# A four-layer decoder on one core: early float8 weights, one-variance norms, full-row biases, and causal masks moved from PE to DVE

## The reference

```python
# l0f: the feed-forward block of layer 0 begins with a norm of a norm, then causal attention
h = layernorm(x);  xn = rmsnorm(h) * ln1          # 32 query heads, 8 key heads of 64
h = h + causal_attention(xn);  y = rmsnorm(h) * ln2
p = softmax(y @ gate_w);  top 2 of 8 experts, their weights renormalised
# l1a: a gated long convolution (Fourier transform written as products), l1f: float8 feed-forward
wq = float8(w); gate, up = xq @ wq_gate, xq @ wq_up; x + float8(act(gate) * up) @ wq_down
# l2a: causal differential attention, 64 query heads of 8 wide; l2f: norm of a norm,
# then causal attention with 16-wide heads, then 7 experts
s = q @ k.T / sqrt(hd);  s = where(k_pos <= q_pos, s, -inf);  softmax(s) @ v
```

## Time and profile before

| | |
|---|---|
| three runs | 2653.11, 2655.5, 2662.68 us; median 2655.5 |
| the profiled execution | 2658.09 us, its span 2656.9 us |
| busy | PE 2081.8 us (78%), DVE 1519.9 (57%), ACT 1089.7 (41%), POOL 1048.7 (39%) |
| stages by time (us from the start) | start and l0a projection 0 to 78, l0a attention to 327, l0x end and l0f norm 343 to 376, l0f attention 388 to 760, router and experts to 1206, l1a 1211 to 1311, l1f 1326 to 1452, l2a 1453 to 1802 (attention 1494 to 1787), l2x to 2172, l2f 2173 to 2440 (attention 2220 to 2312), l3 to 2657 |

### The profile page before, as it was taken

One profiled execution on the slowest core, in us unless ns is written; L12 is line 12 of the kernel. 1 busy time (PEld: TensorE's weight loads), 2 busy tenths in 40 slices (PEclk: granted clock), 3 DMA queues, 4 the chain that ended last, 5 costly groups with the idle time before them and its releaser, 6 DMA issues. The chain is left out here.

```text
span 2656.9 us, 35337 instructions
## 1 busy us (share of the span) xinstructions
PE 2081.8 (78%) x12705; PEld 1444.6 (54%) x12752; DVE 1519.9 (57%) x2932; ACT 1089.7 (41%) x2195; POOL 1048.7 (39%) x1084
## 2 busy tenths in 40 slices
PE   5667759999956888876524988887999978888887
PEld 2333346667646777763302555445687765555446
DVE  6877655545444555544678655544466554456546
ACT  3245625464523434433166144452343434422433
POOL 2766617455636665650254233341232222322000
PEclk8756679999977999997756978888999989979778
DMA  3222110000014445421001000002000000012000
GB/s 140 72 56 59 49 51 8 23 12 16 5 40 155 149 153 163 147 82 44 9 39 37 2 3 2 3 3 103 1 1 1 1 1 1 3 66 107 2 1 17
DMA packets 49150, 121.38 MB, mean 46 GB/s; under 512 B 5553, under 2 KB 18353, under 8 KB 47185
## 3 DMA queue, kind: packets, MB, share of 16 engines
q1 hardware_dynamic: 47440, 114.92, 13.3%
q0 software_dynamic: 1536, 4.20, 0.5%
HBM read 103.50 MB, written 14.55 MB: 44 GB/s over the span
## 5 line engine op out<-in xcount | busy, mean ns | idle before, releaser
L1796 POOL TENSOR_SCALAR l0f_probs<-l0f_probs,l0f_tot 128x128 f32<-128x128 f32 (+1 forms) x256 | 201.6, 806 | 141.8 <-DVE l0f_tot L1743 141.2
L2018 PE MATMUL ps<-l0f_xh,l0f_wh 128*128 128x256 f32 x480 | 149.3, 311 | 49.6 <-DVE l1x_dBu L649 28.4
L1262 DVE TENSOR_REDUCE l2a_a_max<-ps 128x6 f32<-128x768 f32 x128 | 119.4, 953 | 87.5 <-PE ps L1114 86.9
L3114 POOL TENSOR_TENSOR l2x_probs<-l2x_probs,l2x_rc 128x512 f32<-128x512 f32 x64 | 66.5, 1039 | 254.7 <-DVE l2x_rc L3015 254.7
L1318 POOL TENSOR_SCALAR_AFFINE_SELECT l2a_a_probs<-l2a_a_probs 128x256 f32<-128x256 f32 (+1 forms) x192 | 88.3, 484 | 170.4 <-ACT l2a_a_probs L1224 148.3
L2133 POOL TENSOR_TENSOR l0f_wl<-l0f_raw,l0f_wh 128x1024 fp32r<-128x1024 f32 x60 | 141.8, 2375 | 17.8 <-ACT l0f_wh L2058 17.8
L2019 PE MATMUL ps<-l0f_xl,l0f_wh 128*128 128x256 f32 x480 | 141.0, 294 | 0.0
L2020 PE MATMUL ps<-l0f_xh,l0f_wl 128*128 128x256 f32 x480 | 141.0, 294 | 0.0
L1667 ACT ACTIVATE l0f_probs<-ps,l0f_neg 128x128 f32<-128x128 f32 (+1 forms) x256 | 104.3, 424 | 87.2 <-DVE l0f_neg L1733 87.2
L674 POOL TENSOR_TENSOR l1x_y<-l1x_y,l1x_hc 128x512 f32<-128x512 f32 x64 | 80.8, 1283 | 129.0 <-DVE l1x_hc L665 129.0
L2955 ACT ACTIVATE l2x_probs<-ps,l2x_neg,l2x_rs 128x256 f32<-128x256 f32 x128 | 71.0, 559 | 145.5 <-DVE l2x_neg L3005 145.4
(11 more groups left out here) (728 smaller groups left out, 5858.3 us busy)
## 6 DMA issues: line engine op xcount, KB each, us to landing
l0f_raw<-in_e_l0f SPq DMA_DIRECT2D x60, 512.0 KB, 4.1
l0x_bc<-scratch_bc SPq DMA_DIRECT2D x32, 512.0 KB, 4.8
l0f_raw_d<-in_e_l0f SPq DMA_DIRECT2D x60, 256.0 KB, 3.8
scratch_rows<-zero SPq DMA_DIRECT2D x1, 3840.0 KB, 18.8
l0f_xb<-scratch_rows SPq DMA_DIRECT2D x15, 256.0 KB, 4.5
scratch_results<-l0f_yb SPq DMA_DIRECT2D x15, 256.0 KB, 4.8
l0f_slab<-in_g_l0f SPq DMA_DIRECT2D x8, 448.0 KB, 3.5
l1f_raw<-in_w_l1f SPq DMA_DIRECT2D x1, 3072.0 KB, 9.9
```

Of the source, the lines that this page charges most:

```text
L1262: dve.tensor_reduce(M[:, 2 * half:2 * half + 2, j, :], src.rearrange("p a (c n) -> p a c n", c=NB_), AX.X, ALU.max).then_inc(*unit_max.tick())
L1796: last = pool.tensor_scalar(pr[:, u % 3, a, r], pr[:, u % 3, a, r], tot[:, u % 3, qt, a:a + 1], None, ALU.mult)
L2018: pe.matmul(out, hi, xh[:, j % 2, c, :], start=c == 0, stop=False)
```

## The change

Five edits. (1) The causal mask is no longer added on PE. DVE's `tensor_tensor_reduce` adds a mask block to the scores in PSUM, writes them back there, and gives the row's maximum; it is issued four times for each unit, two of 128 columns and two of 256. The products L1114 and L1607, the reductions L1262 (in the causal uses), L1730 and L1731, and `join` go. (2) The float8 rounding of l1_ffn's weights moves into `l1_attention` as class `Early`: four transfers (3 MB) on SP ahead of `dft`, six chunks in each phase between the existing work of ACT, DVE and POOL; mid and round are all on POOL. In the second phase ACT does chunk 6 before it copies the frequencies, 7 to 9 between them and 10, 11 after; DVE scales 6 before K's copies, 7 and 8 after them, 9 after the products of f = 0, 10 and 11 among its last operations; POOL does 6 and 7 before its products and 8 to 11 after. SP stores the result (bf16, 1.5 MB) to `scratch_l1f` before the last barrier, and l1_ffn loads it back. `Turned` writes float8 itself. (3) `NormTwice` gets both norms from one set of statistics, with five operations on 8 or 16 columns and one root. (4) Biases lie in a full block of 128 rows of which the first holds the bias, and are added with a product over 128 rows instead of one. (5) The router of l0f leaves out the division by the softmax's sum, and `start` makes fewer constants.

```diff
+    def masked_max(self, scores, half, out):
+        at = 0 if half else P
+        return self.dve.tensor_tensor_reduce(scores, scores, self.mask[:, at:2 * P], 1.0, 2 * MASKED, ALU.add, ALU.max, out)
...
 start:
-    dve.tensor_copy(k.kb[:, 128:384], k.kf[:, 368:624])
-    dve.memset(k.kb[:, 384:512], 1.0)
-    dve.tensor_copy(k.kb[:, 512:768], k.kf[:, 624:880])
+    dve.memset(k.kb[:, 128:512], 1.0)
...
+class NormTwice:
+    def dve(self):
+...
+        for i in range(NT):
+            dve.tensor_scalar(self.xn[:, i, :], self.src[:, i, :], k.mv[:, i, 0:1], self.both[:, i:i + 1],
+                              ALU.subtract, ALU.mult).then_inc(*k.sig("normed").tick())
+    def dve_first(self):
+        for i in range(NT):
+            k.dve.tensor_scalar(self.h[:, i, :], self.src[:, i, :], k.mv[:, i, 0:1], self.r[:, 0, i:i + 1],
+                                ALU.subtract, ALU.mult).then_inc(*k.sig("v").tick())
...
 project_pe:
-        last = k.pe.matmul(out, k.ones[0:1, :], bias, start=False, stop=True)
+        last = k.pe.matmul(out, k.ones, bias, start=False, stop=True)
...
 small_attention, unit:
-                if causal:
-                    for a in range(2):
-                        diagonal = banks[:, a, :].rearrange("p (q n) -> p q n", n=S)[:, :, 0:P]
-                        last = pe.matmul(diagonal, k.identb, k.mask_qk.unsqueeze(1).to_broadcast([P, 2, P]), start=False, stop=True)
...
 small_attention, largest:
-                src = ring("unit", b, u)[:, :, 0:384] if causal else ring("unit", b, u)
-                dve.tensor_reduce(M[:, 2 * half:2 * half + 2, j, :], src.rearrange("p a (c n) -> p a c n", c=NB_), AX.X, ALU.max).then_inc(*unit_max.tick())
-            def join(b):
-                dve.wait_ge(*unit_max(NU * (b + 1)))
-                dve.tensor_tensor(Mj[:, :, :], M[:, :, :, 1], M[:, :, :, 2], ALU.max).then_inc(*joined.tick())
+                if causal:
+                    for a in range(2):
+                        for qt in range(2):
+                            last = k.masked_max(src[:, a, qt * P:P + qt * S], qt, M[:, 2 * half + a, j, qt:qt + 1])
...
 l0_ffn (and l2_ffn alike):
-                ln.dve(False, 1, collected=True)
-                k.dve.wait_ge(*normed(8))
-                rn.dve(True, 2)
+                norm.dve()
                 turn.dve()
+                norm.dve_first()
...
 l0f_attention, score:
-                for i, (unit, mask) in enumerate(((k.identb, k.mask_qk), (k.ident_swap, k.mask_swap))):
-                    for r, bank in halves:
-                        diagonal = bank[:, 0:512].rearrange("p (q n) -> p q n", n=S)[:, :, 0:P]
-                        last = pe.matmul(diagonal, unit[r, :], mask[r, :].unsqueeze(1).to_broadcast([64, 2, P]), start=False, stop=i == 1)
 l0f_attention, largest:
-                dve.tensor_reduce(m[:, 0, :], banks[:, :, 0:P], AX.X, ALU.max).then_inc(*vc.tick())
-                dve.tensor_reduce(m[:, 1, :], banks[:, :, P:P + S], AX.X, ALU.max).then_inc(*vc.tick())
+                for a in range(2):
+                    for qt in range(2):
+                        k.masked_max(banks[:, a, qt * P:P + qt * S], qt, m[:, qt, a:a + 1]).then_inc(*vc.tick())
...
 router:
-            dve.tensor_reduce(sm[:, :], pr[:, :, :], AX.X, ALU.add).then_inc(*v.tick())
-            dve.reciprocal(sm[:, :], sm[:, :]).then_inc(*v.tick())
-            dve.tensor_tensor(pr[:, :, :], pr[:, :, :], bc(sm), ALU.mult).then_inc(*v.tick())
...
+class Early:
+    CHUNKS, PIECES = 12, ((0, 1), (1, 4), (4, 8), (8, 12))
+    def act(self, i):
+        self.k.act.wait_ge(*self.ready[i])
+        self.quant.act(self.col(self.raw, i), i % 3, i - self.first)
+    def dve(self, i):
+        self.k.dve.wait_ge(*self.ready[i])
+        self.quant.dve_scale(self.col(self.raw, i), i % 3, i - self.first)
+    def pool(self, i):
+        n = i - self.first
+        self.quant.pool_mid(i % 3, n)
+        self.quant.pool_round(self.col(self.raw, i), i % 3, n)
+        self.quant.pool_out(self.col(self.w8, i), i % 3, n)
+    def store(self):
+        self.k.sp.wait_ge(*self.quant.done.now())
+        self.k.sp.dma_start(self.k.kept8, self.w8[:, :]).then_inc(*self.kept.tick())
+        self.k.sp.wait_ge(*self.kept.now())
...
 l1_attention, phase 1 (HERE = 6):
+                early.act(0)
                 for i, (n, dst, off, d, hf) in enumerate(JOBS):
...
+                    if i % 2 == 1 and i // 2 + 1 < HERE:
+                        early.act(i // 2 + 1)
...
+                early.dve(0)
+                early.dve(1)
                 for d in range(2):
                     dve.wait_ge(*taken(2 * d + 2))
                     dve.tensor_scalar(q[:, d], qp[:, d, :, 2:2 + S], w["cqw"][:, d, 2:3], w["cqb"][:, d:d + 1], ALU.mult, ALU.add).then_inc(*v.tick())
+                    if d == 0:
+                        early.dve(2)
+                        early.dve(3)
+                    else:
+                        early.dve(4)
+                        early.dve(5)
...
+            for i in range(HERE):
+                early.pool(i)
...
+            early.store()
             k.barrier()
...
l1_ffn:
-        k.weights("l1f", "l1f", raw)
+        k.load("l1f", w8[:, :], k.kept8)
-            norm, turn = Norm(k, c2, "l1f_", xn, k.x), Turned(k, xT, xn)
+            norm, turn = Norm(k, c2, "l1f_", xn, k.x), Turned(k, x8, xn, saturate=False)
-            dve.tensor_copy(x8[:, :, :], xT[:, :, :], saturate=False)
-            quantise_weights(k, quant, w8, raw, 6144)
```

More of the change, by code:

```diff
@@ L95, in pk, with first_row @@
         return np.ascontiguousarray(np.concatenate(parts, 1))
+    def first_row(b):
+        return np.concatenate([b.reshape(1, -1), np.zeros((P - 1, b.size), np.float32)])
     def ssm(p):
@@ L197, in __init__ @@
         self.identb = self.kb[:, 0:128]
[L198 to L202, removed]
+        self.mask = self.kf[:, 368:624]
         self.w = {}
@@ L357, in act @@
             if self.scale is None:
-                k.act.copy(out, k.ps[:, g, :]).then_inc(*xa.tick())
+                k.act.copy(out, k.ps[:, g, :], **self.cast).then_inc(*xa.tick())
             else:
@@ L368, in dve @@
             if self.scale is None:
-                k.dve.tensor_copy(out, k.ps[:, g, :]).then_inc(*xd.tick())
+                k.dve.tensor_copy(out, k.ps[:, g, :], **self.cast).then_inc(*xd.tick())
             else:
@@ L1109, in unit @@
                         last = pe.matmul(banks[:, a, at:at + w], QT[z][r, j, qt * P:(qt + 1) * P], KT[z][r, hs.kj(j), 0:w],
-                                         start=qt == 0, stop=not causal and qt == 1)
-                if causal:
-                    for a in range(2):
-                        diagonal = banks[:, a, :].rearrange("p (q n) -> p q n", n=S)[:, :, 0:P]
-                        last = pe.matmul(diagonal, k.identb, k.mask_qk.unsqueeze(1).to_broadcast([P, 2, P]), start=False, stop=True)
+                                         start=qt == 0, stop=qt == 1)
                 last.then_inc(*unit_ps.tick())
@@ L1141, in score @@
                         last = pe.matmul(bank[:, i * w:(i + step) * w], KT[z][r, hs.kj(js[i]), kt * P:(kt + 1) * P],
-                                         QT[z][r, js[i]:js[i] + step, q0:q0 + w], start=i == 0, stop=(late or not causal) and i + step == len(js))
-                if causal and not late:
-                    for a in range(2):
-                        diagonal = ps[:, 4 + 2 * (n % 2) + a, :].rearrange("p (j n) -> p j n", n=w)[:, :, 0:P]
-                        last = pe.matmul(diagonal, k.identb, k.mask_kq.unsqueeze(1).to_broadcast([P, len(js), P]), start=False, stop=True)
+                                         QT[z][r, js[i]:js[i] + step, q0:q0 + w], start=i == 0, stop=i + step == len(js))
                 last.then_inc(*scored.tick())
@@ L1871, in step @@
             dve.wait_ge(*v.now())
-        dve.tensor_scalar(self.before[:, :], k.kf[:, 368:496], 0.0, None, ALU.is_lt)
+        dve.tensor_scalar(self.before[:, :], k.kf[:, 496:624], 0.0, None, ALU.is_lt)
         src = pr
@@ L3196, in at_dve @@
                 def at_dve():
-                    ln.dve(False, 1, collected=True)
-                    dve.wait_ge(*normed(8))
-                    rn.dve(True, 2)
+                    norm.dve()
                     turn.dve()
+                    norm.dve_first()
                     for t in range(NT):
```

442 lines of the change are left out of this document (233 added, 209 removed).

## The result

The changed kernel took 2671.6 us in the median of 20 runs (2659.6 to 2680.1), the kernel before 2654.4 (2650.6 to 2669.2). The ratio is 1.0058, 95% interval 1.0043 to 1.0074: slower, by a small but clear 0.6%. I had forecast 2638, faster. The profiled execution has a span of 2677.1 us.

| stretch | before | after | difference | forecast |
|---|---|---|---|---|
| start, to l0a's norm | 15.1 | 13.4 | -1.7 | -1.5 |
| l0a, norm to first score | 64.1 | 61.1 | -3.0 | 0 |
| l0a, first score to l0f's norm | 279.5 | 276.4 | -3.1 | 0 |
| l0f's norms, to its first weights product | 20.4 | 16.4 | -4.0 | -4.1 |
| l0f attention, to the router | 395.0 | 400.6 | +5.5 | -9 |

What follows compares the result with a forecast made beforehand. PE was taken to set the pace in l0f and l2a attention, with waits on DVE's maxima and POOL. Terms summed to -18.5 us (l1_ffn -43.8, l2a +26, phase 1 +13 among them), giving 2638, range 2588 to 2695.

Steps and rivals of the forecast that it cites:

- Net +3.3 us per batch at 1.6: l2a attention: longer DVE maxima outweigh saved PE products if four operations cost 1.6 us; times eight batches, +26 us.
- rival (d): l2a: PE stops more often and is granted the lower clock more, +20 us there, 2658 in all; chance 0.05.
- +0.73 per unit: l2a and l2f: DVE's added time per unit, four masked operations at 1.6 us against one reduction at 0.87.
- my own walk: l2a: one batch followed by its rows, giving about -1 us at 1.2, +3.3 at 1.6, +8 at 2.26.
- an operation of 2.26 us: Masked attentions: four operations cost 2.26 us; l2a +65, l2f +18, l0f +8, 2708 in all; chance 0.22.
- The sign of being wrong: Masks on DVE: forecast wrong if masked_max costs under 1.3 or over 1.95 us, or l2a's stops don't follow it.
- Forecast +6 by DVE: l2f attention: same working as l2a, 4 batches of 8 units, +6 us, from -6 to +18.
- l0f, "-9": l0f attention: PE's saved mask products outweigh DVE's added time, -9 us, from -18 to +8.
- The chain through POOL: l0f: maxima, exponentials, inversion, POOL, then turn; changes by +0.23 us per unit while PE's work falls by 0.32.
- Biases, "0": Bias products: PE streams the same columns whatever the rows, 0 us; bound 4 us from some 40 products.
- Phase 2 itself: l1_attention phase 2: two POOL chunks and early.dve(9) each add 0.8 us, +1.6; up to +5 if cover is gone.
- Phase 1: l1_attention phase 1: early weights' POOL operations hold DVE, plus four scalings of 0.42 us; +13 us, from 9 to 20.

Runs made afterwards that it cites:

- e4: Changed kernel with small_attention's maxima from one reduction over unmasked scores, as cheap as before, and no mask products: 2636.5 us, ratio 0.9900 to the kernel before.
- e6: e4 plus two PE products per unit that add zeros, nothing masked: 2605.3 us, ratio 0.9789 to the kernel before.
- e8: e6 with four zero products per unit; in l0f, DVE's new operation plus four zero products on PE: 2627.7 us, ratio 0.9865 to the kernel before.
- e7: e6 with zero products of 128 columns instead of 256: 2642.3 us, ratio 0.9937 to the kernel before.
- e3: Changed kernel plus two zero-adding PE products per causal unit of small_attention, shaped like the old mask products: 2684.8 us, ratio 1.0086 to the kernel before.
- e10: Changed kernel plus four zero products per unit of small_attention, masks still on DVE: 2645.6 us, ratio 0.9941 to the kernel before.
- e9: e4 with l0f's mask left out altogether, two reductions as before and no mask products; single run: l0f 389.1 us.
- e5: Kernel before with full-row biases alone: 2651.3 us, ratio 0.9974 to the kernel before.

## Why the prediction was wrong

The sum failed at the masks. Point by point:

- **l2a, the step that failed:** "Net +3.3 us per batch at 1.6". I walked the batch with the products' durations of before, that is with their clock of before. The clock is not a constant of the stage. I had the mechanism as rival (d), priced at +20 and at a chance of 0.05, for l2a only, and took the range's upper end from DVE's price. Two errors lay against each other. DVE's price was mis-sized: +0.73 per unit, measured +0.39. By my own walk almost nothing would be lost at 1.26 us, and the stage lost 57. That 2671.6 lies within 2588 to 2695 is luck: the upper part of the range stood for an operation of 2.26 us, which the trace denies. The sign of being wrong that I had named, `masked_max` under 1.3, did come true, at 1.26, but a cheap operation was to make the kernel faster.
- **How the 57 divide.** As a rough estimate, busy PE time times granted clock gives products at full clock: 230 us before, 178 after, so some 52 us of work went. At 0.88 the rest would take 203 us, and it took 283: the clock took back about 80. The measure isn't exact, since the clock is a mean over the whole stretch: the first two zero products per unit raise it by 50 us (e4 to e6), the next two by only 27 (e6 to e8). PE's idle time rose from 37 to 73. The two aren't independent, since slow products delay the maxima. The runs side by side, length and clock, l2a / l2f:

| products per unit | cheap DVE | dear DVE |
|---|---|---|
| none | 318.3 at 0.68 / 105.2 at 0.74 (e4) | 356.0 at 0.63 / 107.3 at 0.76 (after) |
| two zeros of 128 columns | 328.6 at 0.73 / 100.7 at 0.85 (e7) | |
| two of 256 columns | 298.7 at 0.88 / 94.1 at 0.96 (before), 301.2 at 0.87 / 94.1 at 0.96 (e6) | 363.4 at 0.71 / 115.7 at 0.75 (e3) |
| four of 256 columns | 314.8 at 0.90 / 97.1 at 0.96 (e8) | 339.5 at 0.86 / 101.9 at 0.97 (e10) |

The DVE step alone is 25 us of l2a where the clock holds (e8 to e10), 38 where PE is light (e4 to after), and 62 where it tips the clock over at unchanged PE work (e6 to e3). So each half of the change loses the clock by itself. At the measured +0.39 my walk would charge the DVE step some 42 us, which the saved products nearly cancel; measured at a good clock it is 25, and what the walk lacked is that removing the products does not save 45 us but costs 20 (e4).
- **l2f:** the same, 94 to 107. Forecast +6 by DVE; the pair e8 and e10 gives +4.8 for that at a good clock. Removing the products alone gives +11 (e4, clock 0.96 to 0.74), and the DVE step on top of it 2.
- **l0f, "-9":** wrong by itself, and not by the clock (0.97 and 0.95). The forecast set the new 1.6 against the old 1.05, which had the wait before the scaling in it. By the like measure the operation cost 1.41. The chain through POOL was said to take back more than half of the saving; it takes back more than all. No products and cheap DVE give -6 (e9, 389.1). DVE's new operation puts 10 on top: seven profiles have it without the products, six at 398.6 to 400.7 and one (e7) at 395.0. Zero products beside it add 5 (e8). +0.36 us per unit in the chain became +0.16 per unit on the stage, while 0.32 of products gave back 0.09. PE now waits 20.9 us for POOL where the earlier trace rows had 12.8:

```profile
PE ps L1641 <- POOL l0f_probs L1821: 20.9, 15, 2.7
```

- **Biases, "0":** wrong, -7 (e5), beyond the bound of 4 as well. I had said that only the columns count; the one-row products themselves and the full products of the same tiles were slower. Why one row is slower stays open.
- **Right:** the rounding's removal (-43.8, measured -43.6), the norms (-4.1 and -6.0; -4.0 and -6.2), `start`, and the store hidden behind phase 2 (issued at 1306.8, landed after 5.1 us; the last operation ahead of the barrier ended at 1317.4). Phase 2 itself (+1.6; +1.3) came out partly by luck: the biases give back 1.5 in the same stretch (e5), so the early weights cost some 2.8 there. Phase 1 (+13; +11.5) was near, and its mechanism holds. It rests on DVE and POOL taking turns; DVE's and POOL's rows of phase 1 (answer to the earlier trace rows):

```profile
1226.91 2.29 DVE L2465 SCALAR_TENSOR_TENSOR l1a_kv<-l1a_kp,w_l1a,l1a_kv 128x1024 f32<-128x1024 f32 x1
...
1249.60 1.22 DVE L2468 TENSOR_TENSOR l1a_kv<-l1a_kv,l1a_v 128x1024 f32<-128x1024 f32 x1
```

```profile
1214.21 1.26 POOL L2349 TENSOR_TENSOR l1f_early_M<-l1f_early_M,l1f_early_I 128x512 f32<-128x512 f32 x1 [8.88 <-ACT l1f_early_I L2320]
...
1228.09 2.24 POOL L2349 TENSOR_TENSOR l1f_early_M<-l1f_early_M,l1f_early_I 128x512 f32<-128x512 f32 x1
```

DVE's operation of 1.28 us (L2327 before) takes 2.29 beside POOL's, and POOL's of 1.26 takes 2.24. What the prediction lacked: the one-input scalings of the early weights, priced at 0.42, also take longer beside POOL's operations. Five of the twelve took 1.37 to 1.51 us, some 5 us more in all:

```profile
1217.36 1.51 DVE L2327 TENSOR_SCALAR l1f_early_M<-l1f_early_raw 128x512 uint32<-128x512 uint32 x1
```

What stays open is how the chip decides. In l2a the granted clock doesn't follow the columns in proportion (e4, e7, e6: 0.68, 0.73, 0.87), in l2f it nearly does (0.74, 0.85, 0.96). e6 and e7 hold PE's idle time fixed and change its work; no run changed PE's pauses alone without changing DVE's operation.

## What to carry to other kernels

Before you take work from PE in a stage where it isn't full, price what is left at the lower clock as well: here the removed products were what held the clock (0.88 to 0.68). Products that add zero, in the place of the old ones, tell whether it is so, if nothing else differs (e4 and e6). With DVE's dearer operation beside them the same zeros gave no answer (e3), and only twice as many did (e10). And when an operation replaces another in a chain of answers between two engines, count the waits at both clocks, and try the parts of a bundle one at a time: here 1.8% of gain lay under 2.5% of loss.

## What the runs showed that I had not expected

- Removing 256 products, 45 us of work, lengthened l2a by 20 us at equal DVE work; adding them back as zeros took 17 off (e4, e6). Zero products of half the columns were no better than none in l2a (e7, 329), but halfway in l2f.
- The clock fell from 0.87 to 0.73 with PE's idle time the same, 37 and 36 us (e6, e7), and from 0.87 to 0.71 with PE's products the same and DVE's operation dearer (e6, e3).
- A DVE operation with a maximum as second output costs 0.25 us for 128 columns and 0.38 for 256, start to start, its read record of 0.14 us lying almost wholly under the next operation. That is 0.04 over what the earlier trace rows give for the columns alone; ACT's read holds its engine for 0.10.
- A bias product of one row costs 0.41 us for 384 columns where 128 rows cost 0.32, and the four full products of each tile also went faster without it, 1.29 us instead of 1.46 (e5).
